# Attention heads: the loop over batches written out on four engines, waits on constants

## What is computed

```python
# x: (8, 256, 512), mask = cond_2048: (8, 512), 16 heads of 16 features
Q, K, V = (proj(Wq), proj(Wk), proj(Wv))                # (B, 16, 512, 16)
att = jnp.einsum('bhqd,bhkd->bhqk', Q, K) * (1.0 / math.sqrt(Dh))
att = att + b[0]
m = mask[:, None, None, :]
att = att * m + (1.0 - m) * NEG_INF
att = jax.nn.softmax(att, axis=-1)
y = jnp.einsum('bhqk,bhkd->bhqd', att, V)
```

## Time and profile before

| | us |
|---|---|
| median of 3 runs | 3070.81 (3069.7 to 3072.78) |
| the profiled execution | 3071.74 |
| its span, first to last instruction | 3070.0 |
| oscillator and projections, until the first row of `negC` | 1790.1 |
| heads: from there to the last step of the loop | to 2508.5 |
| experts | from 2518.1 |

### The profile page before, as it was taken

How to read it: one execution, slowest core, us unless ns; L and a number is a source line. 1 busy time by engine, 2 the same in 40 slices (tenths; PEclk the granted TensorE clock), 3 DMA queues, 4 the chain that set the end, 5 groups by cost and what they waited for, 6 DMA issues and landing times. The chain is left out here.

```text
span 3070.0 us, 116365 instructions
## 1 busy us (share of the span) xinstructions
PE 2550.0 (83%) x41104; PEld 1785.2 (58%) x41104; DVE 2533.3 (83%) x11914; ACT 1217.3 (40%) x4102; POOL 1352.2 (44%) x3951
## 2 busy tenths in 40 slices
PE   4478888888888888888888778888888876999999
PEld 4356666666666666666667446555655552444444
DVE  7989999999999999999997579989999976544545
ACT  3343333333333333333333368778877760000000
POOL 6846566656666566655563323334333335000000
PEclk6599999999999999999999889999999998999999
DMA  4100000000000000000000431110111110000000
GB/s 180 42 19 10 4 10 10 10 3 10 10 10 10 3 10 10 10 7 7 10 10 10 178 91 34 46 47 25 38 47 43 37 63 8 10 17 27 0 27 14
DMA packets 43922, 88.98 MB, mean 29 GB/s; under 512 B 7168, under 2 KB 23808, under 8 KB 41600
## 3 DMA queue, kind: packets, MB, share of 16 engines
q1 hardware_dynamic: 36336, 63.11, 6.4%
q10 hardware_dynamic: 4752, 10.49, 0.9%
q0 software_dynamic: 2304, 8.39, 0.8%
HBM read 65.18 MB, written 16.78 MB: 27 GB/s over the span
## 5 line engine op out<-in xcount | busy, mean ns | idle before, releaser
L228 PE MATMUL rest<-Tl,CW 128*128 128x56 f16 x16384 | 618.1, 190 | 315.4 <-DVE Tl L494 314.9
L228 PEld LDWEIGHTS rest<-Tl,CW 128*128 128x128 f16 x16384 | 502.6, 97 | 561.2 <-DVE Tl L494 557.5
L347 ACT ACTIVATE Tf<-X 128x32 f32<-128x32 f32 x768 | 176.2, 229 | 779.2 <-DVE X L538 779.2
L1114 DVE CUSTOM_DVE_ANT_0 negL<-Lps,negC 128x512 f32<-128x512 f32 x512 | 339.7, 682 | 43.9 <-PE Lps L1022 42.7
L1032 PE MATMUL Tps<-idS,Pr 128*128 128x128 f32 x2048 | 292.3, 288 | 93.9 <-ACT Pr L1084 87.9
L1134 DVE TENSOR_TENSOR PT<-Tps,PT 128x512 f16<-128x512 f32 x512 | 348.4, 681 | 22.8 <-ACT PT L1091 21.2
L1084 ACT ACTIVATE Pr<-negL,nM 128x512 f32<-128x512 f32 x512 | 358.2, 729 | 17.2 <-DVE nM L1114 16.9
L1091 ACT ACTIVATE PT<-Tps 128x512 f16<-128x512 f32 x512 | 293.0, 597 | 139.9 <-PE Tps L1032 139.8
L625 POOL TENSOR_TENSOR G<-X,Dr 128x32 f32<-128x32 f32 x768 | 207.1, 270 | 300.2 <-DVE X L499 273.2
L1032 PEld LDWEIGHTS Tps<-idS,Pr 128*128 128x128 f32 x2048 | 229.9, 145 | 185.1 <-DVE PT L1134 131.5
L217 PE MATMUL main<-Th,CW 128*128 128x56 f16 x8224 | 264.2, 189 | 10.3 <-DVE CW L450 10.3
(11 more groups left out here) (133 smaller groups left out, 5159.1 us busy)
## 6 DMA issues: line engine op xcount, KB each, us to landing
stage<-w_up SPq DMA_DIRECT2D x8, 1024.0 KB, 4.6
qk<-qkp ACTq DMA_DIRECT2D x32, 256.0 KB, 2.4
QR<-qk SPq DMA_DIRECT2D x128, 64.0 KB, 2.2
KR<-qk SPq DMA_DIRECT2D x128, 64.0 KB, 3.2
wstage<-moe_up POOLq DMA_DIRECT2D x16, 512.0 KB, 5.6
W2m<-w_down SPq DMA_DIRECT2D x1, 4096.0 KB, 13.4
stage<-x_tb SPq DMA_DIRECT2D x16, 256.0 KB, 2.6
x<-stage SPq DMA_DIRECT2D x16, 256.0 KB, 2.1
```

Source lines behind the costliest of these rows:

```text
L228: last = pe.matmul(rest[:, m], CW[:, 0, k, m * P:(m + 1) * P], Tl[:, k:k + 1, :].to_broadcast([P, REP, B]), start=(m == 0 and k == 0), sto ...
L1114: dve.tensor_tensor_reduce(out=negL[:, qt, :], in0=Lps[qt % 2][:, :], in1=negC[:], scale=1.0, scalar=3.0e38, op0=ALU.add, op1=ALU.min, acc ...
```

## The change

`all_heads` runs the 8 batches in a Python loop in place of the loop on the engine. Each of the four engines has 128 heads written out and then the three last steps. `b` is a plain number everywhere, so each wait is on a constant, and the register operations and branches of this loop are gone. In `load_weights` the test for the loop becomes a test for `b > 0`. SP's loop stays.

```diff
--- before.py
+++ after.py
@@ -907,9 +907,7 @@
         def all_heads(eng, step):
 
-            for h in range(NH):
-                step(0, h)
-            with eng.Fori(1, B) as b:
+            for b in range(B):
                 for h in range(NH):
                     step(b, h)
             for h in range(3):
@@ -949,7 +947,7 @@
             def load_weights(b):
 
-                if not isinstance(b, int):
+                if b > 0:
                     pool.wait_ge(moe_lo, 4 * b)
                     pool.sem_inc(halt, 1)
                 for j in range(2):
```

## The result

| | us |
|---|---|
| before, median of 4 runs beside it | 3071.65 (3069.70 to 3072.78) |
| after, median of 4 runs | 3029.48 (3028.33 to 3030.79) |
| ratio, 95% interval | 0.9868 (0.9855 to 0.988) |
| predicted | 3025.8 (3018 to 3044) |
| profiled execution of after, its span | 3030.47, 3028.6 |

A forecast was written before the change was run, and what follows sets the result against it. The prediction took the attention heads to be paced by a PE-ACT cycle, plus stalls at six jumps back. Saving 16.2 + 28.8 = 45.0 us from 3071.74 gave 3026.7, a median of 3025.8 us, range 3018 to 3044.

The forecast's parts named there:

- Term A: Batches 1 to 7: hand-overs between PE and ACT lose register operations, turns go from 5.39 to 5.245 us; 16.2 us.
- Term B: Six jumps back of the heads' loop, 4.8 us each, put down to PE's late branch; 28.8 us go.
- on DVE and POOL these lie off the ring and are worth nothing: In the heads, removing DVE's and POOL's branches and register operations gains 0 us, as the PE-ACT cycle's period covers them.
- the ring: Per head: exponentials on ACT, transposes on PE, fp16 copies on ACT, next exponentials; said to set the pace, 5.25 us.
- The lower bound of B: At the six jumps back, PE's stalls of 3.5 us alone: at least 21 us gained.
- Only the jumps count: Rival: in the heads another engine holds turns at 5.39 us, hand-overs give 0, median 3042.0 us; 7%.
- The edge of a batch costs: Rival: the loss at batch edges comes from new KR, QR and negC and stays; 3053.3 us; 4%.
- Late instructions: Rival: PE's straight-line code for batches 1 to 7 arrives late; 3% slower (3096 us with 20 blocks), 5% for 3036 to 3068.
- nothing, with some 3 us either way: Expert stage: same code at other addresses, so no change expected, give or take some 3 us.
- Sum: Whole kernel: profiled 3071.74 us less 45.0 is 3026.7; median to expect 3025.8 us.
- DVE's limit: In the heads, DVE's 41.39 busy us in eight heads allow no turn under 5.17 us; hand-over gain at most 24.6 us.

The follow-up runs named there:

- the shorter body: Kernel before with its loop kept, PE's body cut by 16 low-half PT products of 32 a head: 3086.76 us, ratio 1.0057.
- The last kernel: Kernel after plus ACT's fourth copy and DVE's fourth subtraction later, sums inverted before the third subtraction, negC double-buffered and computed at head 14: 3016.48 us, ratio 0.9806.

## Why the prediction was right, and where it was not

**Term A, the hand-overs: right.** Forecast 16.2 us. Measured 112 x (5.391 - 5.241) = 16.8, and by parts: PE's side 0.07 us a turn, ACT's 0.08, each shown alone and together with nothing left over. That the constant waits give this is shown; how the 0.07 us splits into the 32 ns of the register operation and what lies around it is not.

**Term B, the jumps: the size right, the reason half wrong.** Forecast 28.8, measured 28.7, as the edges after are plain. But the step "on DVE and POOL these lie off the ring and are worth nothing" was wrong for DVE. Its own jump stalls it as long as PE's does PE, and they lie side by side: take away one and 23 us stay. The 2.89 us that DVE waited for scores were read as the whole of its delay, though its own late code came at about the same time: with PE written out DVE's next work starts 3.5 to 3.7 us behind its branch, and in the kernel before 3.3 to 3.6 us. The sum held only because the change removes both. The lower bound of B (six stalls of PE alone, 21 us) was no bound for the same reason: PE alone gives at most 6. Had the change been to PE only, the same reasoning would have missed by 23 us.

**The rivals.** *Only the jumps count* fell with the turns of 5.24. *The edge of a batch costs* fell with the edges after and with the plain edges inside a body of two batches. *Late instructions* was wrong for the heads: 111 of the 112 turns are plain, and the one of 5.46 us waits for `negC`. The queue of PE's instructions brought 47 blocks between 1880 and 2465 us, where 42 were estimated, against 68 in the loop between 1875 and 2509, here in that order (packets, MB, share):

```profile
q8 instruction: 47, 0.77, 0.5%
```

```profile
q8 instruction: 68, 1.11, 0.7%
```

So the loop did fetch its code again on each pass, which the shorter body did not, and straight-line code needed fewer blocks, not more. The Trainium skill (Runtime: NRT & Kernel Launch, Instruction fetch mechanics) has the crossing of a block mostly hidden in straight-line code, and the trace agrees for these 47, but not for the one in the router.

**The experts: "nothing, with some 3 us either way".** One block was late, outside the stretch that was watched, and the stage takes 1.6 us more (561.75 to 563.34 from the start of the last exponential on). The gap is 2.7 us of that; other things go the other way. The granted clock is among them: a group of the experts takes 126.70 us, or 128.38 where the clock falls at its edge, and how many do differs: two before, one after, none to two over all kept traces. That makes up to 3.4 us, the size of the 3 us either way, for which the prediction gave no row.

**Sum.** Of the 3.7 us between 3025.8 and 3029.48, 2.45 are the later start of the heads, 1.6 the experts, and the 112 turns give 0.4 back. Terms A and B are each right to a microsecond; that the sum is off by 3.7 comes from what it put at nothing, the start of the heads and the experts.

**DVE's limit, used as the upper bound of A, was no limit.** Its 41.39 busy us in eight heads were read as "no turn under 5.17". The last kernel ran turns of 5.10 with the same operations, so its busy time was not all work. In both kernels a subtraction of 0.68 us starts 0.60 us behind the operation ahead of it where nothing holds it, so records overlap by 0.08 us, and a wait of up to that length doesn't show as idle time. With a better order such waits are gone: 5.10 us is what the starts add up to. The eight heads' 41.72 us are also a little less than eight turns of 5.245.

**What stays open.** Registers without any jump were not had, since one trip folds them away; so the two terms are separate by their turns and edges, not by a kernel for each. Why just the block in the router comes late and 47 others don't was not found. The record has a lead that no run tested: in the heads a block lasts PE some 12.4 us (585 / 47), while the router runs through its 384 products and weight loads in 5.15 us, so a block lasts about 3.4 us there (an estimate), little more than the gap itself. The gap is there in every kernel that has PE written out as in the change, and at another product (the 160th) in the one with the shorter body, but not with one trip per loop, nor with code shifted by half a block. DVE's jump with a shorter body was not tried.

## What to carry to other kernels

Look at the branch record of a loop on each engine, and also at the gap ahead of the first work behind it: a long body can make a jump cost 3 us on several engines at once, side by side, and taking it from one of them gains little. A packet on an instruction queue that starts inside such a gap tells that it waits for code. Where a wait depends on a loop's register, see whether the register operation stands behind the semaphore it needs; on a ring between two engines that is paid every turn. And the busy time of a nearly full engine is no floor: ask first which of its operations follow the one they depend on.

## What the runs showed of the hardware

- The price of a taken branch goes with the length of the body, and isn't in the same place on each engine. PE: 0.2 us at 1,350 records, 3.3 to 4.0 at 1,926. DVE, with 537 records: the next work some 3 us late though its record says 63 ns. In each of these stalls a packet on the engine's instruction queue starts 1.0 to 1.5 us behind the branch; with PE's body of 1,350 records there is none for PE. ACT and POOL: the next record 0.26 and 0.28 us behind, and with bodies twice as long 0.53 and 2.6 to 2.9.
- PE with less work was slower: without 256 products a pass the granted clock fell to 1.2 GHz 26 times in the stretch (mean 0.91), with turns of up to 6.6 us away from the edges.
- A boundary of an instruction block can cost 2.5 to 3.2 us of straight-line code on PE (eight kernels), and half a block of other code ahead removes it.
- A dependent operation right behind a reciprocal of 128x4 started 0.28 us behind its start, an independent one 0.09.
